# Softplus moved next to the gate and silu activations in a state-space and dense-layer kernel

## What is computed

```python
x  = einsum('bld,ed->bel', ctx, in_proj_w)              # 512 inner channels
x  = silu(causal_conv4(x) + conv_b)                     # u, per channel
dt_low, B, C = split(einsum('bdl,ed->bel', x, x_proj_w))  # 16 + 16 + 16 rows
dt = softplus(einsum('brl,dr->bdl', dt_low, dt_proj_w) + dt_proj_b)
A  = -exp(A_log)                                        # 512 x 16
# for each position:
dA    = exp(dt[..., None] * A)
state = state * dA + (dt * u)[..., None] * B
y     = einsum('bdn,bn->bd', state, C)
# after the scan:
y = (y + D * u) * silu(layernorm(x_in))                 # the gate
x1  = x_in + y
out = x1 + layernorm(x1) @ (sum of 8 factors) / sqrt(8) + bias
```

## Time and profile before

| | value |
|---|---|
| time, median of 3 runs | 483.33 us (483.25 to 483.36) |
| profiled execution | 482.48 us |
| span of the profiled execution | 480.7 us |
| mean granted TensorE clock | 0.989 |
| busy: DVE, PE, POOL, ACT | 453.5, 432.1, 420.6, 344.7 us |

### The profile page before, as it was taken

How to read it: one execution, slowest core, us unless ns; L and a number is a source line. 1 busy time by engine, 2 the same in 40 slices (tenths; PEclk the granted TensorE clock), 3 DMA queues, 4 the chain that set the end, 5 groups by cost and what they waited for, 6 DMA issues and landing times.

```text
span 480.7 us, 4118 instructions
## 1 busy us (share of the span) xinstructions
PE 432.1 (90%) x1119; PEld 185.3 (39%) x1119; DVE 453.5 (94%) x327; ACT 344.7 (72%) x578; POOL 420.6 (88%) x223
## 2 busy tenths in 40 slices
PE   8799797999979868898989789899979999989996
PEld 5134343434434233333434244343434343344432
DVE  5797999989999999989999999999999899999996
ACT  4669574977659788796869977697879876654422
POOL 4369999998979899997999979797998958999972
PEclk9989999999999989999999999999999999999999
DMA  5799746438982000100694000000396000000002
GB/s 193 267 355 350 200 80 138 83 55 217 292 337 88 1 0 0 42 25 1 191 412 168 0 22 1 0 24 0 132 381 237 1 22 23 22 22 22 0 1 88
DMA packets 16847, 53.96 MB, mean 112 GB/s; under 512 B 1828, under 2 KB 2084, under 8 KB 15800
## 3 DMA queue, kind: packets, MB, share of 16 engines
q1 hardware_dynamic: 15384, 45.14, 25.9%
q0 software_dynamic: 1152, 8.39, 8.8%
q10 hardware_dynamic: 288, 0.18, 0.1%
HBM read 49.24 MB, written 4.46 MB: 112 GB/s over the span
## 4 chain that ended last, share of the span: by engine, by line
POOL 53%; issue 20%; DVE 11%; ACT 6%; PE 4%; DMA 4%; SPq 1%; POOLq 0%; DVEq 0%; ACTq 0%
POOL h L1093 40%; POOL h L1086 9%; DVE dA L946 7%; POOL dtu L1079 3%; DMA c_rep<-bc_scratch 2%; PE y L519 2%; DVE acc L920 2%; ACT dA L776 1%; DMA chan<-channel 1%; DVE h L952 1%; PE work L415 1%; POOL fsum L1123 1%; DVE h L946 1%; ACT gate L690 0%; SPq L331 0%
## 5 line engine op out<-in xcount | busy, mean ns | idle before, releaser
L1093 POOL TENSOR_TENSOR h<-b_rep,dtu 128x1024 f32<-128x1024 f32 x127 | 302.3, 2446 | 12.3 <-DMA b_rep<-bc_scratch 11.3
L519 PE MATMUL y<-h,ident 128*128 128x512 f32 x508 | 236.5, 602 | 34.9 <-DVE h L952 33.0
L946 DVE TENSOR_TENSOR_SCAN dA<-dA,h 128x1024 f32<-128x1024 f32 x97 | 221.8, 2287 | 11.6 <-ACT dA L776 11.1
L776 ACT ACTIVATE dA<-dt,a_neg 128x512 f32<-128x512 f32 x256 | 166.0, 681 | 92.9 <-DVE h L952 76.2
L519 PEld LDWEIGHTS y<-h,ident 128*128 128x128 f32 x508 | 92.8, 190 | 166.2 <-issue 103.7
L952 DVE TENSOR_TENSOR h<-dA,c_rep 128x1024 f32<-128x1024 f32 x96 | 117.1, 1220 | 2.4 <-DMA c_rep<-bc_scratch 0.3
L1086 POOL TENSOR_TENSOR h<-h,c_rep 128x1024 f32<-128x1024 f32 x31 | 74.5, 2403 | 22.3 <-DVE h L946 22.3
L946 DVE TENSOR_TENSOR_SCAN h<-dA,h 128x1024 f32<-128x1024 f32 x31 | 70.6, 2279 | 0.1
L403 PE MATMUL work<-ctx_sb,w_in 128*128 128x512 f32 x60 | 30.6, 644 | 0.3 <-DMA w_in<-w_inT 0.2
L507 PE MATMUL work<-fsum,xnT 128*128 128x512 f32 x64 | 28.8, 592 | 0.0
L920 DVE SCALAR_TENSOR_TENSOR acc<-work,chan,acc 128x511 f32<-128x511 f32 (+2 forms) x30 | 21.6, 731 | 1.3 <-ACT acc L655 1.2
(11 more groups left out here) (128 smaller groups left out, 375.3 us busy)
## 6 DMA issues: line engine op xcount, KB each, us to landing
b_rep<-bc_scratch SPq DMA_DIRECT2D x32, 512.0 KB, 9.7
c_rep<-bc_scratch SPq DMA_DIRECT2D x32, 512.0 KB, 9.3
fsum<-factors POOLq DMA_DIRECT2D x8, 1024.0 KB, 8.3
x<-x SPq DMA_DIRECT2D x4, 1024.0 KB, 7.7
out<-x SPq DMA_DIRECT2D x16, 256.0 KB, 2.0
ctx_sb<-ctxT SPq DMA_DIRECT2D x3, 512.0 KB, 5.7
ctx_sb<-ctxT SPq DMA_DIRECT2D x2, 256.0 KB, 4.4
w_in<-w_inT SPq DMA_DIRECT2D x1, 384.0 KB, 5.2
```

Source lines behind the costliest of these rows:

```text
L519: mm = pe.matmul(y[:], ident[:], h[:, (s * PAIRS + j) % H_RING, i, :], start=False, stop=(j == sum_order(s)[-1] and i == 1))
L776: act.activation(dA[:, j % 2, i, :], dt[:, k % 2, :], ACT.Exp, scale=a_neg[:, k, 2 * j + i:2 * j + i + 1]).then_inc(exp_done, 1)
L946: dve.tensor_tensor_scan(pair if on_pool(s * PAIRS + j) else decay, decay, pair, 0.0, ALU.mult, ALU.add).then_inc(scanned, 1)
L1093: pool.tensor_tensor(h[:, (s * PAIRS + j) % H_RING], b_rep[:, j], dtu[:, k % 2, :].unsqueeze(1).to_broadcast([P, 2, L]), ALU.mult).then_in ...
```

## The change

The slot of the softplus becomes a table by block: after the decays of pair 4 for blocks 0 and 2, after those of pair 2 for blocks 1 and 3 as before. Where a gate or a silu follows in the same slot (blocks 0 of all sequences, and blocks 2 of the first three: steps 0, 2, 4, 6, 8, 10, 12) the exponential table is not loaded after the softplus; the silu table is loaded next, and the load that follows the gate or silu serves both. In step 14 the softplus moves to pair 4 too and keeps its own second load. ACT_TABLE_LOADs over the whole program: 48 before, 41 now. No other engine's program changes.

```diff
-SOFTPLUS_SLOT = 2
+SOFTPLUS_SLOTS = (4, 2, 4, 2)
...
                 is_u, is_g, is_d = nu < STEPS, b + 1 < BATCH, s + 1 < STEPS
+                shared = k == 0 or (k == KB - 2 and b + 1 < BATCH)
...
-                    if j == SOFTPLUS_SLOT and is_d:
+                    if j == SOFTPLUS_SLOTS[k] and is_d:
                         act.preload_act_table_set("softplus")
                         softplus(s + 1)
-                        act.preload_act_table_set("natural_log_exp_and_others")
+                        if not shared:
+                            act.preload_act_table_set("natural_log_exp_and_others")
```

## The result

The changed kernel is slower: 497.69 us in the median (496.61 to 498.25), against 483.35 us, a ratio of 1.0286 with a 95% interval of 1.0262 to 1.0309. That is 14.3 us more. The forecast was 495.3 us, 12.0 us more, with a range to 497.5; the first median lies 0.2 us over the end of that range. The profiled execution took 497.17 us, its span 495.3 us, 14.6 us more than that of before.

A forecast was written before the change was run, and what follows sets the result against it. DVE was taken as the bound: seven pair-5 stalls grow by 13.37 us less 1.34 us returned, 12.03 us, taking the span from 480.7 to 492.7 us and the median from 483.33 to 495.3 us; range 492.3 to 497.5.

The forecast's parts named there:

- The bound: DVE, busy 412.59 of 424 us in the scan, sets the pace; idle time added to it lengthens the end one for one.
- The price: One more load and the softplus between ACT's decays of pairs 4 and 5: 1.91 us per step, 13.37 us over seven.
- what comes back: Earlier decays of pair 4 once the pair-2 burst is gone: 0 to 0.62 us per step, 1.34 us together.
- the seven stalls: DVE's waits for ACT at pair-5 scans of steps 0, 2, 4, 6, 8, 10, 12; 10.09 us before, each to grow.
- The sum: Growth of the seven pair-5 stalls: 13.37 us added less 1.34 us gained, 12.03 us.
- The drain of the table switch: The skill's 1380 ns drain per ACT table switch, unseen in the trace; with it each burst would grow about 3.3 us.
- the 505 us: Estimated whole time, some 505 us, if each ACT table switch also cost the skill's drain.
- The covers: Later softplus delays no PE or POOL work DVE needs; in step 12 PE reaches its product 2.9 us after it.
- Faster through fewer loads: Rival: ACT has no pause between pair 2 and the joint burst, so stalls shrink by 7.74 us, giving 475.6; 5%.
- POOL as the pace of the middle: Rival: DVE has slack from step 4 on, so only steps 0 and 2 count, 3.20 us, giving 486.5; 4%.
- The clock rival: Rival: PE's clock falls in the longer stalls; two falls DVE must wait out add 3.4 us, giving 498.7; 5%.

The follow-up runs named there:

- the softplus was out of the way: Kernel before with the softplus of blocks 0 and 2 one pair earlier, after pair 1, both loads kept, nothing joined: 482.85 us against 483.91, ratio 0.9982.
- filling: Changed kernel plus 28 small zero-adding products on PE in the longer stalls of steps 0, 6, 8 and 12: 495.74 us against 483.91, ratio 1.0245.
- the move alone: Changed kernel's softplus move to pair 4, but the softplus's own exponential load kept everywhere, so as many loads as the kernel before: 507.02 us, ratio 1.0489.
- step 0 put back: Changed kernel with step 0 as in the kernel before, the other six steps joined: 494.7 us, ratio 1.0236.

## Why the prediction was right or wrong

**The bound.** Right. DVE's added waits appeared in the span one for one. In each of the ten profiles after the first, a step is longer or shorter than in the first by what its stall is, to 0.04 us; beyond that only the start up to pair 2 of step 0 differs, and steps 1, 7, 9, 11 and 13, by 1.8 us at most. In the windows of the changed kernel, DVE is busy for 412.64 of the 439 us from 46 to 485, as for 412.59 of 424 before: the same work, with the new gaps in between.

**The price and what comes back.** Right, and closely: the seven stalls were forecast at about 4.5, 3.6, 2.6, 2.9, 2.6, 2.9 and 3.1 us and measured at 4.49, 3.62, 2.63, 2.88, 2.63, 2.87 and 3.13. The sum of 12.03 us was 12.16. The terms were also measured apart: the price of 1.91 us in steps 0 and 8, where nothing comes back (1.92 and 1.91), the return at 1.27 us for 1.34, and the load at 1.27 to 1.29 us in each step. ACT's busy time fell by 9.1 us in the second profile, for 9.0; in the first it fell by 8.2, as other activations took some 0.8 us longer there.

**The drain of the table switch.** The Trainium skill (ScalarE: Activation LUTs, section "What ACT_TABLE_LOAD costs") adds a drain of 1380 ns to the load at each switch of tables. In the burst above every load is followed by the next instruction 1.29 us after its start, and begins 0.02 or 0.03 us after the end of the one ahead. The measurement decides: no such drain here, and the 505 us by it did not come.

**The covers.** They held. In step 12 the softplus ended at 384.97 and PE reached its product at 387.87, the 2.9 us of the forecast. PE's x_proj did wait for the silu, 3.4 us in all, which it did not before; no wait of DVE can be laid to it in the first profile.

**The rivals.** Faster through fewer loads: refuted by the result itself, and by what came back when the softplus was out of the way, 1.27 us in all. POOL as the pace of the middle: refuted, since each of steps 4, 6, 8, 10 and 12 grew by 1.7 to 1.9 us. The chain of work that ended last would have misled, and not only as evidence for this rival: it differs between two executions of one program. In the first profile of the changed kernel DVE has 38% of it and POOL 8%. This is the second, and then the second of the kernel before, where POOL had 53% in the first:

```profile
POOL 49%; issue 23%; DVE 11%; DMA 6%; PE 4%; ACT 4%; SPq 2%; POOLq 0%; DVEq 0%; ACTq 0%
...
DVE 40%; issue 20%; PE 14%; ACT 14%; POOL 7%; DMA 3%; SPq 1%; DVEq 0%; POOLq 0%; ACTq 0%
```

The seven stalls were the same in both profiles of each kernel. This fits the prediction's remark that the chain follows the later of two signals that come almost together.

**What failed.** The clock rival was put aside at 5%, with the argument that the one fall shown of before cost DVE nothing, and the sum has no term for it. It came true in part. Step 7 took 28.12 or 28.13 us, 1.70 us more, in three of the four profiles of kernels with the long stalls and no filling (the second of the changed kernel, the move alone, step 0 put back), and 26.42 or 26.43 us in the fourth and in all seven others. The falls in step 13 cost 1.25 us in one profile of the changed kernel and nothing in the other. The prediction looked for the damage in the windows of the fall itself, where DVE was full. It arises behind them, where ACT or DVE needs PE's result at a fixed place: DVE's first longer wait in step 7 ends at 239.75 us, some 6 us after the 4 us of the fall shown. The size given, 3.4 us for two falls, was about right (2.95 us); it should have widened the range rather than stand outside it with 5%.

The medians lie 2.3 and 1.7 us above the sum. The two falls of one profile (2.95 us) and the late start of the other (2.5 us) are each of about that size, but which of them an execution without a profile had is not shown. That they are common in the changed kernel is likely from the mean granted clocks, 0.962 to 0.979 in its eight runs against 0.979 to 0.993 in all runs of the kernel before.

**DVE's busy time** rose from 453.5 to 455.0 instead of staying: the one slow instruction at the start. In the second profile of the changed kernel, where that took 0.22 us, it was 453.6.

## What to carry to other kernels

Before joining two bursts on an engine that runs ahead of the bound engine, compare the length of the joined burst with the lead that the buffers between them give. In this kernel a burst below that length was free, and what went beyond it was paid in full. Work that is removed where the lead covers it anyway buys nothing, and a longest burst can be split although that adds loads. Where stalls grow, look also behind them for a fall of TensorE's clock, and at what is due from it at a fixed place. And before a difference of two traces is laid to a change, profile each kernel a second time: here the start, the falls and the chain of work all differed between two executions of one program.

## What had not been expected of the hardware

A fall of TensorE's clock at the start of step 7 shows in one profile of the changed kernel and not in the other, with the same program, although PE was busy for the same 2.02 of the 4 us ahead in both. In the two profiles of the kernel before PE was busy for 2.30 and 2.17 of the same 4 us, and no fall came. DVE was busy throughout these 4 us in all four, so the pause of PE that precedes the fall does not lie in DVE's stall. Why the clock fell at one time and not at another no run here shows.

A DVE instruction on 128 x 4 elements took 0.17 us in one execution and 1.66 us in another of the same kernel, early in the program while the scan's rows were being loaded, and between 0.17 and 2.35 us over the eleven profiles; what held it up is open. The whole start up to the product of pair 2 varied by 2.9 us between executions, which is a third of the 9 us that seven table loads are worth.
